# Low parts of the second norm's copied rows: from VectorE to GpSimd, at the end of its slot

## What is computed

```python
def layer(h, p):
    q = phi(h @ wq + bq); k = phi(h @ wk + bk); v = h @ wv + bv      # 16 heads of 8
    kv = einsum('bshd,bshm->bhdm', k, v)
    z = 1 / (einsum('bshd,bhd->bsh', q, k.sum(axis=1)) + 1e-6)
    h = ln(h + einsum('bshd,bhdm,bsh->bshm', q, kv, z) @ wo + bo, g1, be1)
    return ln(h + gelu(h @ w1 + c1) @ w2 + c2, g2, be2)
x = x + ln(scan(layer, layernorm(x)), gf, bef)
x = x + experts(layernorm(x))       # softmax router, top 2 of 8, silu between two matmuls
```

## Time and profile before

| | |
|---|---|
| median of 3 runs | 1076.96 us (1074.14 to 1085.29) |
| the profiled execution, its own time | 1077.69 us |
| its span | 1076.0 us |
| mean granted TensorE clock | 0.970 |
| slots 6 to 26 (175 to 680 us) | 24.8 us each, 26.3 us where bias products stand in it |

### The profile page before, as it was taken

How to read it: one execution, slowest core, us unless ns; L and a number is a source line. 1 busy time by engine, 2 the same in 40 slices (tenths; PEclk the granted TensorE clock), 3 DMA queues, 4 the chain that set the end, 5 groups by cost and what they waited for, 6 DMA issues and landing times.

```text
span 1076.0 us, 25009 instructions
## 1 busy us (share of the span) xinstructions
PE 999.4 (93%) x7558; PEld 934.7 (87%) x7558; DVE 822.2 (76%) x2710; ACT 833.0 (77%) x1621; POOL 771.3 (72%) x1157
## 2 busy tenths in 40 slices
PE   5799899999999999999999999999998859989983
PEld 5698798999999999999999999899997759889983
DVE  6666788888888888888888888877889888953514
ACT  6767788888888888888888888888886745765572
POOL 5958777777767777777777777777766677677752
PEclk9899899999999999999999999999999878999997
DMA  4101134325512531443244315501100345667784
GB/s 139 50 2 35 32 81 89 59 42 111 107 37 63 121 58 38 94 92 59 41 99 89 60 41 117 106 17 21 21 1 2 92 129 165 175 199 214 209 257 156
DMA packets 198499, 94.65 MB, mean 88 GB/s; under 512 B 120124, under 2 KB 179523, under 8 KB 198368
## 3 DMA queue, kind: packets, MB, share of 16 engines
q1 hardware_dynamic: 193824, 84.59, 32.9%
q0 software_dynamic: 4544, 8.47, 2.3%
HBM read 44.82 MB, written 29.44 MB: 69 GB/s over the span
## 4 chain that ended last, share of the span: by engine, by line
PE 71%; POOL 7%; DVE 7%; issue 5%; ACT 3%; DMA 3%; SPq 3%; POOLq 0%; DVEq 0%
PE psum L1904 18%; PE psum L1781 8%; PE psum L1783 7%; PE psum L1782 7%; PE psum L1828 5%; PE psum L2061 5%; PE psum L1834 5%; PE psum L1862 5%; PE psum L2045 5%; PE psum L1816 4%; SPq L498 2%; ACT s L1009 1%; POOL xs L912 1%; DVE stat L1215 1%; POOL rstd L741 1%
## 5 line engine op out<-in xcount | busy, mean ns | idle before, releaser
L1009 ACT ACTIVATE s<-s,shift,rstd 128x128 f32<-128x128 f32 x496 | 203.9, 486 | 48.2 <-POOL shift L743 48.0
L1904 PE MATMUL psum<-this_w,hid 128*128 128x128 f32 x1792 | 217.3, 278 | 1.1 <-DMA this_w<-w 1.0
L1904 PEld LDWEIGHTS psum<-this_w,hid 128*128 128x128 f32 x1792 | 209.5, 194 | 1.7 <-DMA this_w<-w 1.6
L988 ACT ACTIVATE hid<-psum,col 128x512 f32<-128x512 f32 x256 | 155.7, 684 | 3.5 <-PE psum L1783 3.3
L741 POOL TENSOR_TENSOR rstd<-var,neg_half 128x4 f32<-128x4 f32 x132 | 145.0, 1098 | 11.0
L784 POOL TENSOR_TENSOR res_a<-s,row 128x512 f32<-128x512 f32 x60 | 77.6, 1293 | 86.2 <-ACT s L1009 80.9
L1215 DVE BATCH_NORM_STATS2 stat<-s 128x6 f32<-128x128 f32 x512 | 109.9, 275 | 0.0
L1781 PE MATMUL psum<-x_hi,this_w 128*128 128x512 f32 x224 | 96.3, 430 | 0.7 <-DVE x_lo L1287 0.7
L769 POOL TENSOR_TENSOR res_f<-res_f,row 128x512 f32<-128x512 f32 x64 | 92.4, 1443 | 5.0
L2061 PE MATMUL psum<-heads,hid 128*128 x624 | 86.3, 283 | 6.0 <-ACT hid L1141 5.7
L738 POOL TENSOR_SCALAR shift<-mv 128x4 f32<-128x4 f32 x132 | 26.6, 202 | 90.4 <-DVE mv L1219 89.4
(11 more groups left out here) (264 smaller groups left out, 2738.6 us busy)
## 6 DMA issues: line engine op xcount, KB each, us to landing
xs<-pad SPq DMA_DIRECT2D x18, 975.0 KB, 8.3
feature<-xrow SPq DMA_DIRECT2D x416, 32.0 KB, 2.0
res_a<-w SPq DMA_DIRECT2D x40, 256.0 KB
xblk<-xs SPq DMA_DIRECT2D x78, 65.0 KB
raw_w<-w SPq DMA_DIRECT2D x18, 256.0 KB, 2.8
row<-rows SPq DMA_DIRECT2D x8, 512.0 KB, 5.2
this_w<-next_w SPq DMA_DIRECT2D x7, 512.0 KB, 3.2
third_w<-w SPq DMA_DIRECT2D x10, 256.0 KB, 6.7
```

What stands on the lines that cost most here:

```text
L988: a.activation(hid[h][:, c, :], ps(3 + h + c), ACT.Gelu, bias=col[:, bass.ds(lw * FF + (C_C1 + c), 1)]).then_inc(hid_done, 1)
L1009: ins = a.activation(dst[:, t, :], src[:, t, :], ACT.Identity, bias=shift[i][:, t:t + 1], scale=rstd[i][:, t:t + 1])
L1904: ins = t_.matmul(ps(down_bank(l, s, h))[:, t * P:(t + 1) * P], hid[h][:, c, t * P:(t + 1) * P], down[:, c, :], start=c == 0, stop=c == FF ...
```

## The change

GpSimd gets `lo_moved`. It stands behind scale_resid(1) for h=0 and behind offset_resid(1) for h=1; resid_a(1) is taken apart for that. DVE no longer has it. Two waits come with it: since xt_lo_done is now raised by two engines, each low part on POOL waits until the ones before it in the count are done, and DVE's lo_xt (the two flipped slots) does the same. In the slot with index 26 (l=6, s=2) lo_xt(0) thereby waits for POOL's lo_moved(1) of the pair of slot 23, which stands in the same slot.

```diff
@@ POOL
+            def lo_moved(l, s, h):
+                wait(pool, xt_hi_done, flipped_upto(l, s, h))
+                wait(pool, xt_lo_done, flipped_upto(l, s, h) - 1)
+                u = half_at(l, s, h)
+                g.tensor_tensor(xt_lo[:, u], feature[:, h, :], xt_hi[:, u].bitcast(F32),
+                                ALU.subtract).then_inc(xt_lo_done, 1)
+
             def slot(l, ring, s, first, last):
...
                     offset_resid(l, s - 2, 0)
-                    resid_a(l, s - 2, 1)
+                    scale_resid(l, s - 2, 1)
+                if swapped(l, s - 3):
+                    lo_moved(l, s - 3, 0)
+                if p2:
+                    offset_resid(l, s - 2, 1)
+                if swapped(l, s - 3):
+                    lo_moved(l, s - 3, 1)
                 if first and s == 0:
                     router_constants()
@@ DVE
             def lo_xt(l, s, h):
                 wait(dve, xt_hi_done, flipped_upto(l, s, h))
+                wait(dve, xt_lo_done, flipped_upto(l, s, h) - 1)
                 low_part(half_at(l, s, h), 4 + h)
-
-            def lo_moved(l, s, h):
-                wait(dve, xt_hi_done, flipped_upto(l, s, h))
-                u = half_at(l, s, h)
-                d.tensor_tensor(xt_lo[:, u], feature[:, h, :], xt_hi[:, u].bitcast(F32),
-                                ALU.subtract).then_inc(xt_lo_done, 1)
...
                 if turns:
                     turn(l, s - 2, 0)
-                if swapped(l, s - 3):
-                    lo_moved(l, s - 3, 0)
-                    lo_moved(l, s - 3, 1)
                 if flips:
                     lo_xt(l, s - 2, 0)
```

## The result

| | before | after |
|---|---|---|
| median of 4 runs each | 1078.35 us | 1110.13 us (1108.61 to 1114.16) |
| ratio, 95% interval | 1 | 1.0292 (1.026 to 1.0324) |
| profiled execution: span | 1076.0 | 1112.4 |
| slots s=0, 1, 2, 3 (P0 to next P0) | 24.8, 24.8, 26.33, 24.8 | 26.02, 26.15, 26.83, 25.96 |

A forecast was written before the change was run, and what follows sets the result against it. PE was taken as the bound. Stalls of 22.9 and 3.0, 2.3 for slot l=0, s=3 and 4.7 for l=6, s=2, less 3.0 coming back, make 29.9 us: 1107 us against the median, range 1094 to 1122.

The forecast's parts named there:

- P0: Start of the first matmul of project(h=0) in a slot on PE, which waits for xt_lo.
- PE is the bound, DVE's relief worth 0: PE is busy 502.10 of 505.00 us from 175 to 680 us, so taking L1319 off DVE gains 0.
- The price of one: One lo_moved on POOL takes L731's 1273 ns, starts 1.24 us apart; bounds 630 ns and 1.72 us.
- sigma: Start of POOL's scale_resid(1) (L784), behind which the moved instructions are queued; 1.33 us ahead of P0 in one slot.
- P0 waits for what is queued behind sigma: Earliest P0 is sigma+2.56; PE's stalls are 22.9 us over 21 slots, plus 3.0 in three more.
- The four kinds of slot: Distance from sigma to P0 is 2.26, 1.33, 1.11 and 0.94 us ahead of s=3, 0, 1 and 2, setting each stall.
- What comes back: With PE waiting, DVE's kt and the next sigma come earlier after P0: 0.2 us in 15 slots, -3 us.
- The P1 stall: P1, the start of project(h=1), comes 2.48 us after P0 instead of 2.19; absorbed where the next P0 waits.
- Slot l=6, s=2: DVE's lo_xt waits for lo_moved(1), so PE's start of project(h=1) goes from 710.32 to 715.0: 4.7 us.
- The first slots: Slot 3 to 6: 3.8 us more, 2.3 of it for slot l=0, s=3, where POOL is already late.
- The queue behind lo_moved(1): POOL's inv_std1(0) comes 0.1 to 0.7 us late, taken up by POOL's idle time: price 0, at most 7 us.
- POOL becomes the bound: Rival, chance 0.08: POOL's loop grows 2.48 us in each of 26 slots, making inv_std1(1) late: 64 us, 1141.

The follow-up runs named there:

- e5_no_low: Kernel before, each moved low part cut to one column of 512 on DVE, none on GpSimd: 1079.04 us, ratio 0.9976.
- e8_free_end: e1_early with sum_rows and hi_w1 taken from the ends of their slots to the middle: 1085.65 us, ratio 1.0052.
- e1_early: Changed kernel with both lo_moved on GpSimd ahead of scale_resid(1): 1088.64 us, ratio 1.0111.
- e7_late: Changed kernel with both lo_moved behind offset_resid(1): 1149.11 us, ratio 1.0639.
- e4_both_ahead: Changed kernel with lo_moved(1) also ahead of offset_resid(1), both directly behind scale_resid(1): 1110.31 us, ratio 1.029.
- e2_slot26_dve: Changed kernel, but the low parts of the pair of slot 23 stay on DVE: 1103.59 us, ratio 1.0199.
- e3_h1_only: Changed kernel, but lo_moved(0) stays on DVE and only lo_moved(1) is on GpSimd, behind scale_resid(1): 1084.91 us, ratio 1.0053.
- e6_spare: Kernel before, plus two unused same-shape subtractions on GpSimd at the change's two places: 1096.31 us, ratio 1.0123.

## Why the prediction was right

- *PE is the bound, DVE's relief worth 0.* By e5_no_low the time falls by 0.24% (interval 0.01 to 0.46%), with the plain slots no shorter; e8_free_end, with all of the work off DVE, has them no shorter either.
- *The price of one.* 1281 ns mean over 52, by start-to-start spacing 1.23, where I took L731's 1273 and 1.24. The longest took 1311, so none ran at the 1.72 of the upper bound. P0 came at sigma+2.55 (forecast 2.56); in the slots s=0 it was 2.64, with lo_moved(0) at its usual 1.23 behind sigma, and why is open. The Trainium skill's rule of "Perfetto Trace Analysis", GPSIMD Engine Instruction, to go by spacing, held where it can be read: lo_moved(0) starts 1.23 behind scale_resid(1), whose own span is 1.27. The 2.61 that the prediction gives for spans is that of two instructions, scale_resid(1) and lo_moved(0), not of four.
- *P0 waits for what is queued behind sigma.* Shown from both sides: earlier in the queue (e1_early) the waits are gone, one instruction later (e7_late) each P0 is 1.34 later. There are 24 such P0s in the prediction's sum (21 and 3), where it also speaks of 23. In the change 23 waited: ahead of slot 6 sigma lay 4.93 before P0, since slot 5 had been long for another reason.
- *The four kinds of slot.* Forecast more per slot, after 0.2 of return: about 1.0, 1.25, 1.4 for those with P0 ahead of s=0, 1 and 2, and 0.3 ahead of s=3. Measured by slot length: 1.16 (slot s=3), 1.2 (s=0), 1.35 (s=1), 0.5 (s=2). The slots s=2 are the ones with the new wait of 0.28 for norm1(0).
- *What comes back.* DVE starts kt 2.40 to 2.44 after P0 (2.6 in the slots s=3) instead of 2.69, and the next sigma is 23.47 and 23.60 after P0 instead of 23.70 and 23.84 in the slots s=0 and s=1 (0.24), 23.31 for 23.45 in s=3 (0.14); I had taken 0.2 and bounded it by 0.32. In the slots with sum_rows nothing comes back, there sigma is 0.2 later (24.28 for 24.08).
- *The P1 stall is absorbed.* P1 at 2.50 (forecast 2.48). That its loss changes nothing is seen in the slots s=1 and s=3 of e4_both_ahead, where P1 and flip_x1(0) come 0.3 earlier and the next P0 does not.
- *Slot l=6, s=2.* 5.1 for 4.7; e2_slot26_dve gives 4.9. P1 came at 741.61 though DVE was done at 741.30: the rest was PE, at 0.63 per matmul after its wait of 3.13. The wait of DVE for POOL, for which I had named some 5 us, was 7.54: DVE now came to it without the 1.6 us of its own two low parts, and lo_xt(0) had stood 1 us ahead of sigma before.
- *The first slots.* 6.1 for 3.8. Of the 2.3 too many, 1.0 is a longer wait for a weight DMA in slot 5 (1.98 against 0.99) and the rest matmuls at a lower granted clock behind it (0.86 over the last 11.8 us of that slot); e4_both_ahead has neither, and takes 3.9 more from slot 3 to 6; e2_slot26_dve, whose code there is the change's, takes 1.9 more. So this stretch differs by some us between executions, and what is above the forecast can't be laid to the change.
- *The queue behind lo_moved(1), price 0.* This is the weakest step. L738 came at 2.4, 2.9 and 3.4 after P0, forecast 2.4, 3.1 and 3.3, and in the change the price was 0 but for the slots s=2, where PE waited 0.28 us for norm1(0) and the next sigma came 0.2 later. It was that small because the waiting P0 gives POOL the time: e1_early, e3_h1_only and e6_spare have the whole load or a part of it in that queue without the wait, and lost 6.2, 3.4 and 12.4 us from slot 6 to 26. So a loss by POOL's load was hidden under the cause that I named. It is not the rival "POOL becomes the bound" as I had put it: that one went by inv_std1(1) in every slot, 64 us, while what is seen goes by inv_std1(0), norm1(0) and flip_x1(0), and most of it in the slots s=0 and s=2. The two losses don't add up: in the change a waiting P0 covers most of the second. That the total came within 3 us of the forecast rests in part on this cover, for which the prediction had only the argument that "the P0 stall itself gives POOL time".

## What to carry to other kernels

An instruction that is moved to another engine is due at its reader's time, not when the engine has room: write down the time of the instruction that it is queued behind, add the queue, and compare it with the reader's start; here that gave the loss to 2 us, while busy shares (72% on the receiving engine) said nothing. Then look at what stands behind it in the new queue, as well, and at a moment when its reader does not wait, because a stall can cover a second one. If the engine in front is 99% busy, the relief of any other is worth measuring by leaving the work out once, before it is moved.

## What was not expected of the hardware

A stall of PE can cost more than its length. In e7_late 20 of the waits at P0 were 2.0 to 2.7 us long; 9 of them were followed by a granted clock of 0.57 to 0.69 over 4 us, with matmuls at 0.63 instead of 0.40, and between slots 6 and 26 the slots were 1.1 to 1.6 us longer than their like; 11 were not, with waits of 2.3 to 2.7 us. In e6_spare it came behind two of five waits of 1.92 us. In the changed kernel, whose plain waits are at most 1.3 us, it was not seen in any of those slots, only behind the waits of 3.13 and 1.98 us named above. And GpSimd's two-input subtraction of 128x512 took 1.04 us when both inputs were one constant tile read four times over (e6_spare), 1.27 with two full tiles; what in that makes the difference was not tried.
